# One-hot products with folded tables for q, k and v in a fused token, attention and expert kernel

## What is computed

```
combined = concat([pos_table[s], nest_table[nesting], seg_table[segments]])
h   = combined @ W                              # 32 x 512 x 128
xn  = (h - mean(h)) / sqrt(var(h) + eps)
qkv = xn @ qkv_w.T + qkv_b                      # 8 heads of 16
h   = h + softmax(q k^T / 4) v @ out_w.T + out_b
xn2 = layernorm(h)
w   = gates of 4 experts from softmax and sigmoid of xn2, cut at 0, normalised
h   = h + sum_e w_e * (relu(xn2 fc1_e^T) loA_e loB_e fc2_e^T)
```

## Time and profile before

| | |
|---|---|
| median of 3 runs | 1201.24 us (1200.89 to 1202.33) |
| the profiled execution | 1200.39 us, span 1198.6 us, mean granted clock 0.973 |
| busy: PE, DVE, ACT, POOL | 1112.8, 910.2, 823.0, 592.8 us |

### The profile page before, as it was taken

The page is one execution under the profiler, slowest core; times in us unless marked ns, Lnnn a source line. Parts: engine busy times, 40 slices in busy tenths (PEclk is TensorE's granted clock), DMA queues, the critical chain, the costliest instruction groups (busy, mean ns, idle before and its releaser), DMA issues.

```text
span 1198.6 us, 20409 instructions
## 1 busy us (share of the span) xinstructions
PE 1112.8 (93%) x6392; PEld 455.6 (38%) x6392; DVE 910.2 (76%) x2370; ACT 823.0 (69%) x1602; POOL 592.8 (49%) x588
## 2 busy tenths in 40 slices
PE   2579999999999999999999999999999999999975
PEld 1223334444344434434344444443443444433322
DVE  6288888877888788777888887778888877788322
ACT  0217777777777777777777777777777777777841
POOL 2644555456544555565445655654455555622231
PEclk9669999999999999999999999999999999999997
DMA  3534534545454345454444455444444454441111
GB/s 84 130 81 97 123 88 113 120 110 123 103 120 105 102 106 119 116 120 105 117 107 102 102 120 125 111 107 114 112 102 100 118 127 109 109 102 44 54 56 36
DMA packets 88377, 123.98 MB, mean 103 GB/s; under 512 B 17469, under 2 KB 69054, under 8 KB 82054
## 3 DMA queue, kind: packets, MB, share of 16 engines
q1 hardware_dynamic: 86720, 121.08, 43.0%
q10 hardware_dynamic: 1550, 1.59, 0.5%
HBM read 80.81 MB, written 34.95 MB: 97 GB/s over the span
## 4 chain that ended last, share of the span: by engine, by line
PE 59%; DVE 20%; issue 4%; DMA 1%; POOL 1%; ACT 0%; SPq 0%; POOLq 0%; DVEq 0%
PE pv L635 14%; PE mix L645 12%; PE sc L624 11%; DVE negmax L882 11%; PE mix L697 7%; PE mix L662 4%; PE mix L713 3%; PE mix L702 2%; PE mix L680 2%; PE mix L657 2%; DVE out_sb L961 2%; DVE rden L901 1%; PE mix L673 1%; DVE onehot L861 1%; DVE mres L892 1%
## 5 line engine op out<-in xcount | busy, mean ns | idle before, releaser
L882 DVE TENSOR_REDUCE negmax<-mix 128x1 f32<-128x512 f32 x1024 | 669.9, 680 | 173.3 <-PE mix L645 166.2
L507 ACT ACTIVATE probs<-sc 128x512 f32<-128x512 f32 x1024 | 576.8, 598 | 183.8 <-PE sc L624 179.4
L624 PE MATMUL sc<-qstk,kstk 120*128 120x512 bf16 x1024 | 366.8, 381 | 0.8 <-ACT probs L507 0.6
L645 PE MATMUL mix<-kstk,qstk 96*128 96x512 bf16 x1024 | 357.2, 392 | 10.0 <-DVE negmax L882 4.8
L635 PE MATMUL pv<-probs,vals 128*32 128x512 f32 x2048 | 274.0, 601 | 0.0
L645 PEld LDWEIGHTS mix<-kstk,qstk 96*128 96x128 bf16 x1024 | 99.7, 98 | 347.2 <-DVE negmax L882 198.1
L460 POOL TENSOR_TENSOR ctxh<-ctx_sb,rdenb 128x512 f32<-128x512 f32 x64 | 81.3, 1271 | 258.7 <-DMA rdenb<-rden_dram 258.2
L624 PEld LDWEIGHTS sc<-qstk,kstk 120*128 120x128 bf16 x1024 | 99.5, 98 | 106.1 <-issue 36.6
L697 PE MATMUL mix<-xn2T,fc1T_sb 128*128 128x512 f32 x256 | 131.9, 599 | 0.0
L416 POOL TENSOR_TENSOR hb_sb<-h_sb,obias 128x512 f32<-128x512 f32 x32 | 40.7, 1273 | 121.6 <-DVE h L907 121.6
L565 ACT ACTIVATE hid<-mix 128x512 f32<-128x512 f32 x128 | 76.8, 600 | 24.2 <-PE mix L697 24.2
(11 more groups left out here) (116 smaller groups left out, 1067.8 us busy)
## 6 DMA issues: line engine op xcount, KB each, us to landing
stack_dram<-pieces SPq DMA_DIRECT2D x192, 128.0 KB
rdenb<-rden_dram SPq DMA_DIRECT2D x64, 256.0 KB
qstk<-stack_dram SPq DMA_DIRECT2D x32, 384.0 KB, 6.6
kstk<-stack_dram SPq DMA_DIRECT2D x32, 384.0 KB, 8.7
qstk<-stack_dram SPq DMA_DIRECT2D x32, 256.0 KB, 6.9
kstk<-stack_dram SPq DMA_DIRECT2D x32, 256.0 KB, 9.3
wrow<-w_dram SPq DMA_DIRECT2D x32, 256.0 KB
out<-out_sb SPq DMA_DIRECT2D x32, 256.0 KB, 2.7
```

The costliest lines, as they stand in the source:

```text
L507: act.activation(probs[:, c % 8, i % 2], sc[:, i % RING], ACT.Exp).then_inc(s_exp, 1)
L624: pe.matmul(sc[:, i % RING, :], kstk[0:KROWS, u, h, j * P:(j + 1) * P], qstk[0:KROWS, u, h, :], start=True, stop=True).then_inc(s_score, 1)
L645: pe.matmul(max_bank(m), qstk[0:STK, u, h, j * P:(j + 1) * P], kstk[0:STK, u, h, :], start=True, stop=True).then_inc(s_mxmm, 1)
L882: dve.tensor_reduce(negmax[:, m // NT, m % NT:m % NT + 1], max_bank(m), AX.X, ALU.max, negate=True).then_inc(s_max, 1)
```

## The change

q, k and v no longer come from the normalised, turned activations. The mean's removal and the token weights are linear, so the setup folds them into the tables: `table` grows from 128 to 4 x 128 columns (embedding, q, k, v), and position parts `posQK` and `posV` are computed in the setup. In the loop, PE multiplies the one-hot with a bf16 table for q, k and v; what is still missing is the position part and 1/sigma, which for q and k lies along the free axis. So 1/sigma goes to DRAM in 4-byte elements (`rstd_out`) and comes back spread over 128 partitions (`rstd_in`). ACT copies q and k out (`raw`), POOL adds the positions and multiplies (`scale`), and ACT adds the bias in place and casts as before (`qk`). v is copied by ACT into `v32`; POOL adds the positions and multiplies (`v`). `norm`, `xnT` and ACT's copies into `vals` are gone. The product slots are filled anew: v in slot 1, the first expert's `fc1_0` in slot 9, `fc1_1` in 10, `fc1_2` and `fc1_3` in 13 and 14, and slot 15 has none.

```diff
 PRODUCTS = [
-    ("project", -2), ("xnT", 3), ("q", 3), ("low", -3), ("k", 3), ("xn2T", -2), ("out", -3), ("gates", -2),
-    ("turn_gates", -2), ("v", 3), ("fc1_0", -2), ("embed", 4), ("mT", 1), ("fc1_1", -2), ("fc1_2", -2), ("fc1_3", -2),
+    ("project", -2), ("v", 3), ("q", 3), ("low", -3), ("k", 3), ("xn2T", -2), ("out", -3), ("gates", -2),
+    ("turn_gates", -2), ("fc1_0", -2), ("fc1_1", -2), ("embed", 4), ("mT", 1), ("fc1_2", -2), ("fc1_3", -2), ("none", None),
 ]
 ACT_WORK = [
-    (1, 1, "xnT", 3, 0), (2, 1, "qk", 3, 0), (4, 0, "ctx", -1, 1), (4, 2, "qk", 3, 1), (5, 2, "xn2T", -2, 0),
-    (8, 0, "gates", -2, 0), (9, 0, "gate_exp", -2, 0), (9, 1, "v", 3, 0), (10, 1, "relu", -2, 0),
-    (12, 0, "mT", 1, 0), (12, 0, "ctx", 0, 0), (12, 1, "wT", -2, 0), (13, 1, "relu", -2, 1), (14, 1, "relu", -2, 2),
-    (15, 1, "relu", -2, 3),
+    (2, 1, "v", 3, 0), (2, 2, "raw", 3, 0), (4, 2, "raw", 3, 1), (4, 0, "ctx", -1, 1), (5, 1, "qk", 3, 0), (5, 2, "xn2T", -2, 0), (6, 2, "qk", 3, 1),
+    (8, 0, "gates", -2, 0), (9, 0, "gate_exp", -2, 0), (9, 1, "relu", -2, 0), (10, 1, "relu", -2, 1),
+    (12, 0, "mT", 1, 0), (12, 0, "ctx", 0, 0), (12, 1, "wT", -2, 0), (13, 1, "relu", -2, 2), (14, 1, "relu", -2, 3),
 ]
 POOL_WORK = [
-    ("add_bias", 3, 0), ("rstd2", -2, 0), ("norm2", -2, 0), ("second", 3, 0), ("residual", 3, 0), ("third", 3, 0),
-    ("second", 3, 1), ("residual", 3, 1), ("third", 3, 1), ("normalise", -1, 0), ("rstd1", 4, 0), ("norm", 4, 0),
+    ("add_bias", 3, 0), ("rstd2", -2, 0), ("norm2", -2, 0), ("scale", 3, 0), ("scale", 3, 1),
+    ("second", 3, 0), ("residual", 3, 0), ("third", 3, 0), ("second", 3, 1), ("residual", 3, 1), ("third", 3, 1),
+    ("v", 3, 0), ("normalise", -1, 0), ("rstd1", 4, 0),
 ]
 SP_WORK = [
-    ("ids", 4, 0), ("piece", 3, (0, 0)), ("den_out", -1, 1), ("piece", 3, (0, 1)), ("piece", 3, (0, 2)),
-    ("den_in", -1, 0), ("piece", 3, (1, 0)), ("piece", 3, (1, 1)), ("out", -3, 0), ("piece", 3, (1, 2)),
-    ("rden_out", -1, 0), ("rden_in", -1, 0), ("den_out", 0, 0), ("max_in", 1, 0), ("weights_out", -2, 0),
-    ("weights_in", -2, 0), ("stack", 3, 0), ("stack", 3, 1),
+    ("ids", 4, 0), ("den_out", -1, 1), ("den_in", -1, 0), ("piece", 3, (0, 0)), ("piece", 3, (0, 1)),
+    ("out", -3, 0), ("rden_out", -1, 0), ("piece", 3, (0, 2)), ("piece", 3, (1, 0)), ("rden_in", -1, 0),
+    ("piece", 3, (1, 1)), ("piece", 3, (1, 2)), ("den_out", 0, 0), ("max_in", 1, 0), ("weights_out", -2, 0),
+    ("rstd_out", 4, 0), ("weights_in", -2, 0), ("rstd_in", 4, 0), ("stack", 3, 0), ("stack", 3, 1),
 ]
...
+            def store_rstd(b):
+                upto(sp, s_rstd1, b)
+                upto(sp, s_rstdin, b - 1, 16)
+                sp.dma_start(rstd_dram.rearrange("(j p) -> p j", p=P), rstd1[:],
+                             allow_slow_non_contiguous=True).then_inc(s_rstdout, 16)
+
+            def load_rstd(b):
+                upto(sp, s_scaled, b - 1, 2)
+                upto(sp, s_rstdout, b, 16)
+                sp.dma_start(rstdb[:], rstd_dram.partition_broadcast(P)).then_inc(s_rstdin, 16)
...
+            def scale(b, side):
+                upto(pool, s_raw, b, 2, side + 1)
+                pool.tensor_tensor(qk32[:, side, :], qk32[:, side, :], posQK[:, side, :], ALU.add).then_inc(s_sum, 1)
+                upto(pool, s_sum, b, 2, side + 1)
+                upto(pool, s_rstdin, b, 16)
+                pool.tensor_tensor(qk32[:, side, :], qk32[:, side, :], rstdb[:], ALU.mult).then_inc(s_scaled, 1)
...
-            def copy_xnT(b):
-                upto(act, s_xnTmm, b)
-                upto(act, s_vmm, b - 1)
-                act.copy(xnT[:], aux("xnT", 1)).then_inc(s_xnT, 1)
-
+            def copy_raw(b, side):
+                upto(act, (s_qmm, s_kmm)[side], b)
+                upto(act, s_pc1, b - 1, 2, side + 1)
+                upto(act, s_res0, b - 1, 2, side + 1)
+                act.copy(qk32[:, side, :], aux("qk"[side], 1)).then_inc(s_raw, 1)
...
+            pe.wait_ge(s_fold, 4)
+            pe.matmul(sc[0:HOT, 0, 0:3 * P], catWT, qkvC.rearrange("p i n -> p (i n)"), start=True, stop=True).then_inc(s_fold2mm, 1)
+            for side in range(2):
+                pe.matmul(sc[:, 1 + side], qkvC[:, side], posWT, start=True, stop=True).then_inc(s_fold2mm, 1)
+            for j in range(NT):
+                mm = pe.matmul(mix[:, 3, j * P:(j + 1) * P], posWT[:, j * P:(j + 1) * P], qkvC[:, 2], start=True, stop=True)
+            mm.then_inc(s_fold2mm, 1)
...
             def v(b):
-                upto(pe, s_xnT, b)
+                upto(pe, s_hot, b)
                 for j in range(NT):
-                    mm = pe.matmul(aux("v")[:, j, :], xnT[:, j * P:(j + 1) * P], qkvT_sb[:, 2, :], start=True, stop=True)
+                    mm = pe.matmul(aux("v")[:, j, :], onehot[:, j * P:(j + 1) * P], table[:, 3], start=True, stop=True)
                 mm.then_inc(s_vmm, 1)
```

More of the change, by code:

```diff
@@ L167, in tower @@
         rstd1 = sb("rstd1", [P, NT])
-        hc = sb("hc", [P, NT, P])
-        xn = sb("xn", [P, NT, P])
-        xnT = sb("xnT", [P, S])
+        rstdb = sb("rstdb", [P, S])
+        v32 = sb("v32", [P, NT, NH, HC])
         qk32 = sb("qk32", [P, 2, S])
@@ L213, in tower @@
         low = sb("low", [P, S])
+        centre = hid[:, 0, 384:512]
+        qkvT_sb = hid[:, 0, 0:384].rearrange("p (i n) -> p i n", i=3)
+        qkvC = hid[:, 1, 0:384].rearrange("p (i n) -> p i n", i=3)
+        posWT = hid[:, 2, :]
+        catWT = hid[:, 3, 0:HOT]
         out_sb = sb("out_sb", [P, NT, P])
@@ L387, in _ @@
                 "out": lambda b, u, _: store_out(b),
+                "rstd_out": lambda b, u, _: store_rstd(b),
+                "rstd_in": lambda b, u, _: load_rstd(b),
             }
@@ L467, in _ @@
             pool.wait_ge(s_const, 3)
+            pool.wait_ge(s_pos, 3)
             work = {
-                "rstd1": lambda b, u, _: rstd(b, mv1, ve1, rstd1, s_mv1, s_ve1, s_rstd1, s_xn, 1),
-                "rstd2": lambda b, u, _: rstd(b, mv2, ve2, rstd2, s_mv2, s_ve2, s_rstd2, s_xn2, 1),
+                "rstd1": lambda b, u, _: rstd_first(b),
+                "rstd2": lambda b, u, _: rstd_second(b),
+                "scale": lambda b, u, side: scale(b, side),
+                "v": lambda b, u, _: value(b, u),
                 "residual": lambda b, u, side: residual(b, side),
@@ L497, in _ @@
             act.wait_ge(s_qb, 1)
+            act.wait_ge(s_foldmm, 1)
+            act.copy(posWT, sc[:, 0]).then_inc(s_fold, 1)
+            act.wait_ge(s_foldmm, 2)
+            act.copy(catWT, sc[:, 1, 0:HOT]).then_inc(s_fold, 1)
+            act.wait_ge(s_foldmm, 3)
+            act.mul(qkvC[:, 0], sc[:, 2, 0:P], QSCALE).then_inc(s_fold, 1)
+            act.copy(qkvC[:, 1:3], sc[:, 2, P:3 * P].rearrange("p (i n) -> p i n", i=2)).then_inc(s_fold, 1)
+            for side in range(2):
+                act.wait_ge(s_fold2mm, 2 + side)
+                act.copy(posQK[:, side, :], sc[:, 1 + side]).then_inc(s_pos, 1)
+            act.wait_ge(s_fold2mm, 4)
+            act.copy(posV[:], mix[:, 3].rearrange("p (j n) -> p j n", j=NT)).then_inc(s_pos, 1)
             act.wait_ge(s_const, 4)
@@ L517, in copy_qk @@
                 upto(act, s_res0, b - 1, 2, side + 1)
[L518 to L519 removed]
+                act.copy(qk32[:, side, :], aux("qk"[side], 1)).then_inc(s_raw, 1)
+            def copy_qk(b, side):
+                upto(act, s_scaled, b, 2, side + 1)
+                act.activation(qk32[:, side, :], qk32[:, side, :], ACT.Identity,
+                               bias=(qb_sb[:], qkb_sb[:, 1:2])[side]).then_inc(s_qk32, 1)
                 upto(act, s_qk32, b, 2, side + 1)
@@ L568, in _ @@
                 "qk": lambda b, u, side: copy_qk(b, side),
-                "v": lambda b, u, _: copy_v(b, u),
+                "v": lambda b, u, _: copy_v(b),
+                "raw": lambda b, u, side: copy_raw(b, side),
                 "xn2T": lambda b, u, _: copy_xn2T(b),
@@ L629, in values @@
                 g, half = r // 2, r % 2
+                if r == 0 and jj == 0:
+                    upto(pe, s_v, b, 2)
                 if jj == 0:
@@ L650, in embed @@
                 for j in range(NT):
-                    mm = pe.matmul(aux("embed")[:, j, :], onehot[:, j * P:(j + 1) * P], table[:], start=True, stop=True)
+                    mm = pe.matmul(aux("embed")[:, j, :], onehot[:, j * P:(j + 1) * P], table[:, 0], start=True, stop=True)
                 mm.then_inc(s_embmm, 1)
```

115 lines of the change are left out of this document (68 added, 47 removed).

## The result

The changed kernel takes 1510.94 us (1508.74 to 1513.15) beside 1201.07 us for the kernel before on the same chip: a ratio of 1.258, with a 95% interval of 1.2554 to 1.2606. The forecast was 1185 us, range 1158 to 1210. The sign is wrong and the time lies 300 us outside.

What follows compares the result with a forecast made beforehand. PE was taken to bound most of a step, DVE slots 7 to 11. First steps +16, 26 steps at -1.2 (-31) and last two -1 turn 1200.4 into 1184, as a median 1185 us; range 1158 to 1210.

Steps and rivals of the forecast that it cites:

- The trip of `rstd_out`: Store of 1/sigma to DRAM, ahead of the stacks: taken as 4.5 us, between 2.3 and 6.4.
- the bound above: Upper estimate for the 1/sigma store: 512 packets at 95 ns, 32 per engine, with a longer issue, 6.4 us.
- covered by POOL's wait of 7.43 us before `normalise`: POOL's added work for q, k and v, +5.4 us a step, fits its idle wait; costed at 0.
- The denominators' rival: `den_out` sits behind stacks and `rstdb`, stopping DVE's slot 7 reciprocal and PE; 1224 us at 1.7 late; chance 0.20.
- I am wrong if DVE waits for `den`: Stated sign in the profile after that would refute the forecast: DVE waiting for the reloaded denominators.
- The stacks' arithmetic: Stack loads start at the next `project`'s end; the last lands at most 14.2 us after, slot 8 wants it at 15.1.
- Just enough: Verdict on the last stack load: 14.2 us after `project`, against 15.1 when slot 8 wants it.
- The first steps: Setup and first sequences: first scores of step 0 at about 106.5 instead of 90.84, +16 us, bounds 8 and 22.
- The forecast's own terms: First maxima tile at 71 instead of 51.13, 4 taken back by sequence 0's maxima, sequence 1's stacks 2 late.
- PE's work: Cheaper products in PE's stretch, slots 15, 1, 2 and 4: -2.36 us a step before waits for banks.
- the ring: Tiles in slots 1 to 6 wait for ACT's copies: 0.5 us gained there, 1.37 a step with slot 15.
- v's copy at slot 2: PE waits near 1 us for ACT's copy of v at the second tile of slot 2.

Runs made afterwards that it cites:

- run 4: The kernel before with an unused store and spread load of 1/sigma, 512 elements of 4 bytes: 1445.22 us, ratio 1.2037.
- run 8: The kernel before with the unused trip of 1/sigma, its store in 128 rows of 16 bytes: 1219.37 us, ratio 1.0142.
- run 14: The kernel before with an unused store of 128 4-byte elements side by side, the spread load reading an input row: 1377.26 us, ratio 1.1477.
- Run 1: The changed kernel without the store and reload of 1/sigma, a constant in its place for q and k: 1329.44 us, ratio 1.108.
- run 9: The changed kernel without 1/sigma's trip and POOL's q/k scaling, v behind `normalise`, ACT's casts in slots 3 and 5: 1160.91 us, ratio 0.966.
- Run 10: The kernel before with only v as one-hot product, in slot 15, its POOL work outside slots 7 to 9, no trip: 1183.65 us, ratio 0.9847.

## Why the prediction was wrong

Two terms failed, each enough to turn the sign.

- **"The trip of `rstd_out`": 4.5 us taken, 6.4 as the bound above; 8.3 on empty queues, 10.8 in a step.** The bound came from a count, 512 packets at 95 ns. The count was right: the queue has 21504 packets more, 12288 of them (run 4 against run 8) the store's 512 elements in place of 128. But most of the time is not in the count, as run 14 shows, and no row of before had elements of 4 bytes side by side. The rule of the Trainium skill that was weighed there (DMA: Bandwidth & Descriptors, Rules for kernel authors), one descriptor for each element, told the count and a remedy that works, but not the time; a bound by the count alone was too low.
- **POOL: "covered by POOL's wait of 7.43 us before `normalise`", cost 0.** POOL's own time was right: 763.1 - 592.8 = 170 us, 5.3 a step, forecast 5.4, and `normalise` was not late by it. But the wait of the earlier trace rows was not free time. It was the stretch in which DVE, which sets the end of slots 7 to 12, had its small operations without POOL beside it. Run 1 has 1067.8 us of DVE busy and run 9 914.2: 4.8 us a step. Behind a DVE that is late PE's `fc1_0` takes 2.07 in place of 0.86, another 1.2. Their steps differ by 5.9 (38.6 and 32.7), so these two are nearly all of it. The prediction asked what POOL's work delays in the order of waits, and never what runs beside it.
- **The denominators' rival was the right mechanism at the wrong size.** It named the place, SP behind stacks and DVE's reciprocal, and the sign ("I am wrong if DVE waits for `den`"), but gave it 0.20 and priced it at 1224 us, for a fixed lateness of 1.7 us a step. In the traces it feeds itself: late denominators make a late 1/sigma, which makes late stacks, and a step is 9 us longer (run 4, without the rest of the change: 7).
- **The stacks' arithmetic fell with the trip.** "Just enough" (14.2 against 15.1 us) became a wait of PE for `kstk` of 130.8 us in 31 steps.
- **The first steps: +16 forecast, +40 measured.** The forecast's own terms (71 - 51.13, 4 back, 2 late) add up to 18. `embed` at 26.47 was right (27). The three trips took 8.26, 8.90 and 10.32 in place of 4.5 each, 14 of the 24 us missed, and the spread load 5.53 in place of 3.45.
- **PE's work and the ring were right**, but only run 9 could show it: 1.4 us less a step for 1.37, with each of the four tiles within 0.02 us of its forecast. PE waits 0.73 us for v's copy at slot 2 there; forecast was near 1.

The shares by the runs, taken in this order: without the trip 181 us come back; without POOL beside DVE another 168 (run 1 to run 9, which also leaves out POOL's scaling); what stays is a gain of 40 us, in a kernel that leaves out the trip and the scaling of q and k. What stays open: why neighbouring elements of 4 bytes are slow to store; how DVE's two-input operations behave beside a POOL that only writes; and whether all of q and k could be had this way with POOL's four added operations placed clear of DVE's. No such kernel was tried. Run 10 takes v alone, which needs no trip.

## What to carry to other kernels

A wait in one engine's timeline is only cover for new work if nothing that sets the end runs on an engine beside it and shares something with it: before filling GpSimd's idle stretch, look at what DVE does in it, and put the work where DVE does reductions or operations that read PSUM, which kept their lengths here (`finish`, 128x512, took 0.69 us in run 1 beside POOL's 1.16 as it did before). A small store took its time here from the layout of its elements, far more than from its bytes or their number; give each partition 16 bytes in a row, or keep 4-byte elements apart, and never let bulk loads stand behind its landing. Where a late transfer feeds the work that issues the next one, price a loop and not a delay.

## What the runs showed of the hardware that was not expected

- A store of 128 elements of 4 bytes took 7.5 us where they lay side by side in DRAM and 1.6 where they lay 512 bytes apart; of 8 bytes each 4.0, of 16 bytes 1.8. The Trainium skill (DMA: Bandwidth & Descriptors, Specifications) says that transfers under 512 bytes are done by read-modify-write; all of these are under it, and they differ by more than a factor of four, so that alone doesn't tell their time.
- DVE's casts, its one-input operation `gsel` and its operations with two inputs in SBUF, of 4 to 32 elements a partition, went from 0.2 to 1.1 us and more beside GpSimd instructions of 1.16 us and ended within 0.04 us of them; its reductions and reciprocals did not. GpSimd's kept their length where they came first; one that came 0.03 us after DVE's one-hot took 1.43 us in place of 1.26. Memsets on GpSimd held up DVE's casts as well.
- A small transfer that came behind the stack loads was slow from either of the two queues tried: the denominators' store took 7.15 us from SP's and 5.06 from ACT's, their reload 7.15 in place of 1.71.
